# A ternary feed-forward kernel: low rank product in two bank pairs, copies and norms reordered, last rows by halves, masks of the second weight on GpSimd

## The reference

```python
def bitlinear(x, w):                       # per output row of w
    scale = clip(mean(abs(w), axis=1), 1e-5)
    tern = clip(round(w / scale), -1, 1)
    return x @ (tern * scale).T

def attn(x):       # 16 heads of 64, keys: 4 sinks and the last 512 tokens, causal against them
    w = softmax(where(cols <= rows + (t_ctx - t), q @ k.T / 8, -inf)); w = where(isnan(w), 0, w)
    return (w @ v) @ Wo

x = x + layernorm(attn(layernorm(x)))
h = bitlinear(layernorm(x), w_fc) + gate * (layernorm(x) @ v.T @ fast_b.T @ u.T)
x = x + layernorm(bitlinear(relu(h) ** 2, w_proj))
```

## Time and profile before

| | us |
|---|---|
| median of 3 runs | 1091.73 |
| lowest, highest | 1087.86, 1093.29 |
| the profiled execution | 1087.22 |
| its span, on the slowest of 8 cores | 1085.6 |
| spans of the other cores | 1078.3 to 1085.5 |

### The profile page before, as it was taken

How to read it: one execution, slowest core, us unless ns; L and a number is a source line. 1 busy time by engine, 2 the same in 40 slices (tenths; PEclk the granted TensorE clock), 3 DMA queues, 4 the chain that set the end, 5 groups by cost and what they waited for, 6 DMA issues and landing times.

```text
span 1085.6 us, 15004 instructions; the slowest of 8 cores (1078.3 to 1085.6 us)
## 1 busy us (share of the span) xinstructions
PE 1007.6 (93%) x4933; PEld 457.8 (42%) x4933; DVE 564.8 (52%) x817; ACT 362.4 (33%) x697; POOL 40.3 (4%) x97
## 2 busy tenths in 40 slices
PE   2789767999999899999999999999999989999997
PEld 1233233444444344544544444445444444444443
DVE  3877968744654553553445344633445354544333
ACT  4688787531002431134211341123310232014200
POOL 0101112000000000000000000000000000000000
PEclk9998889999999999999999999999999999999999
DMA  8799779841453314620445134522144301311021
GB/s 267 178 259 265 201 200 217 188 105 59 142 158 93 99 48 107 162 51 7 74 111 125 46 45 79 154 59 65 46 110 136 78 21 30 114 51 40 1 72 45
DMA packets 106223, 116.93 MB, mean 108 GB/s; under 512 B 82317, under 2 KB 82573, under 8 KB 106148
## 3 DMA queue, kind: packets, MB, share of 16 engines
q1 hardware_dynamic: 102180, 103.64, 36.9%
q0 software_dynamic: 3728, 12.25, 5.9%
q10 hardware_dynamic: 240, 0.07, 0.0%
HBM read 87.79 MB, written 17.31 MB: 97 GB/s over the span
## 4 chain that ended last, share of the span: by engine, by line
PE 81%; DVE 5%; DMA 5%; issue 4%; ACT 3%; SPq 1%; POOL 0%; ACTq 0%; DVEq 0%; POOLq 0%
PE pjp L635 37%; PE fcb L618 30%; PE pjp L618 3%; DVE below L1393 1%; PE xp L781 1%; PE xp L635 1%; PE xp L744 1%; PE pt L618 1%; PE fcb L635 1%; ACT rpp L1012 1%; PE xp L681 1%; DMA lrow<-ctx 1%; ACT absd L1052 1%; DMA stg<-wfc 1%; DMA r<-v 1%
## 5 line engine op out<-in xcount | busy, mean ns | idle before, releaser
L618 PE MATMUL fcb<-xnT,Sfc 128*128 128x512 bf16 x1792 | 408.0, 385 | 9.9 <-DVE r L1369 9.4
L635 PE MATMUL pjp<-Spj,r 128*128 128x512 fp8e4 x1664 | 366.8, 380 | 1.7 <-DVE r2b L1369 1.7
L618 PEld LDWEIGHTS fcb<-xnT,Sfc 128*128 128x128 bf16 x1792 | 172.2, 99 | 226.0 <-issue 34.4
L1369 DVE TENSOR_TENSOR r<-fcb,rpp 128x512 bf16<-128x512 f32 x192 | 131.3, 690 | 217.9 <-ACT rpp L1012 217.7
L635 PEld LDWEIGHTS pjp<-Spj,r 128*128 128x128 bf16 x1664 | 160.8, 98 | 195.9 <-issue 7.3
L1012 ACT ACTIVATE rpp<-fcb,hsc 128x512 f32<-128x512 f32 x192 | 130.4, 686 | 210.1 <-PE fcb L618 201.1
L975 ACT ACTIVATE lv<-mv,cvecs 128x1 f32<-128x1 f32 x64 | 18.8, 293 | 286.2 <-DVE mv L1342 206.5
L1332 DVE TENSOR_TENSOR xy<-pjp,oscb 128x512 f32<-128x512 f32 x60 | 41.3, 689 | 132.4 <-PE pjp L635 132.4
L635 PE MATMUL pjp<-Spj,r2b 128*128 128x512 fp8e4 x256 | 55.4, 379 | 0.0
L1337 DVE BATCH_NORM_STATS2 s<-xy 128x6 f32<-128x512 f32 x64 | 44.4, 694 | 9.4 <-DVE xy L1332 6.1
L618 PE MATMUL pjp<-xnT,Sfc 128*128 128x512 bf16 x176 | 41.9, 388 | 7.0 <-ACT xnT L992 3.7
(11 more groups left out here) (166 smaller groups left out, 681.5 us busy)
## 6 DMA issues: line engine op xcount, KB each, us to landing
out<-xy SPq DMA_DIRECT2D x32, 512.0 KB, 2.9
xy<-x SPq DMA_DIRECT2D x31, 512.0 KB, 4.5
xs<-x SPq DMA_DIRECT2D x25, 512.0 KB, 4.6
xy<-wfc SPq DMA_DIRECT2D x16, 512.0 KB, 5.8
xy<-wpj SPq DMA_DIRECT2D x15, 512.0 KB, 5.3
stg<-wfc SPq DMA_DIRECT2D x10, 512.0 KB, 6.4
stg<-wpj SPq DMA_DIRECT2D x9, 512.0 KB, 5.4
xs<-wpj SPq DMA_DIRECT2D x8, 512.0 KB, 5.0
```

Of the source, the lines that this page charges most:

```text
L618: mm = te.matmul(bank, s_fc[:, dci * HF + hc * 128:dci * HF + hc * 128 + 128], xnT[:, dci * TT:(dci + 1) * TT], start=(dci == 0), stop=(dc ...
L635: mm = te.matmul(dst, squares(j)[:, hc * TT + s * 128: hc * TT + s * 128 + 128], spj_even[:, hc // 2, hc % 2, half * 512:half * 512 + 512] ...
L1369: ve.tensor_tensor(squares(j)[:, hc * TT:(hc + 1) * TT], bank, rpp[n % 2][:], ALU.mult).then_inc(v_r2, 1)
```

## The change

- The low rank product alternates between `xp` and `pjp` by unit, so that it waits for the mask two units back and not for the last one. `low_rank(1)` moves ahead of `turn(3)`; TensorE's wait for all masks moves from row block 7 to 4, whose transposes use `pjp`.
- Tile 0: ScalarE takes `rstd1(3)` ahead of `turned(2)`, VectorE `cut(0)` between the statistics and the apply step of block 3.
- Tile 1: `turned(4)` to `turned(7)` move to the head of n = 33.
- Second weight: GpSimd's `under(n)` makes the mask of units 32 to 63, between its `group` calls, with a wait for the ternary step of unit n-2; VectorE waits for it.
- Ring: units from 49 on use slots 5 to 8 and 0 to 3, sums run 7 units ahead from 49 and 6 from 57; tile 1's chunks: 16 between n = 37 and 47, then 49, 51, 53, 55, and 56 to 59 as before.
- `stats` loses its wait; the apply steps `ln_end` and `residual_end` run from `attend_end`.
- Last block: VectorE normalises columns 0 to 511, ScalarE 512 to 1023, VectorE adds x by halves, SyncE stores by halves.

```diff
@@ -38,10 +38,9 @@
 NUNIT = NFU + NPU
 GRP = 4
 NSLOT = 9
-NRING9 = 58
-
-SLOT = [n % NSLOT if n < NRING9 else (6, 7, 8, 0, 1, 2)[n - NRING9]
-        for n in range(NUNIT)]
+
+SLOT = [n % NSLOT for n in range(49)] + [5, 6, 7, 8, 0, 1, 2, 3,
+                                         6, 7, 8, 0, 1, 2, 3]
 TURN_OF = [SLOT[:n].count(SLOT[n]) for n in range(NUNIT)]
 USERS = [[n for n in range(NUNIT) if SLOT[n] == k] for k in range(NSLOT)]
 AFTER = {n: m for u in USERS for n, m in zip(u, u[1:])}
@@ -53,14 +52,14 @@
 TURN_AT = [16 * len([m for m in range(n % 3, n + 1, 3) if m not in BY_PE])
            for n in range(NUNIT)]
 SUMS = [[u for u in range(8, NUNIT)
-         if u - (8 if u < NRING9 else 6) == n] for n in range(NUNIT)]
+         if u - (8 if u < 49 else 7 if u < 57 else 6) == n] for n in range(NUNIT)]
 CHUNKS = [[] for n in range(NUNIT)]
 for c in range(24):
-    CHUNKS[36 + 11 * c // 12 if c < 12 else 35 + c if c < 20 else 36 + c
+    CHUNKS[37 + 11 * c // 16 if c < 16 else 17 + 2 * c if c < 20 else 36 + c
            ].append(c)
 LATE = range(24, HCN)
 
-PLACE = {12: 49, 16: 50, 20: 58, 24: 63}
+PLACE = {12: 40, 16: 49, 20: 57, 24: 63}
 
 STATS = {25: 4, 26: 5, 27: 6, 28: 7}
 
@@ -133,6 +132,8 @@
         lv2 = sbuf("lv2", [128, NI], F32)
         rs1 = sbuf("rs1", [128, NI], F32)
         rs2 = sbuf("rs2", [128, NI], F32)
+
+        nmean = sbuf("nmean", [128, 2], F32)
         wsum = sbuf("wsum", [128, NUNIT], F32)
         thr = sbuf("thr", [128, NFU + OCN], F32)
         nthr = sbuf("nthr", [128, NFU + OCN], F32)
@@ -276,6 +277,7 @@
         g_us = sem("g_us")
         v_rt = sem("v_rt")
         g_own = sem("g_own")
+        g_be = sem("g_be")
         p_ut = sem("p_ut")
         a_ut = sem("a_ut")
         v_ab = sem("v_ab")
@@ -328,6 +330,8 @@
         v_y2 = sem("v_y2")
         a_y2 = sem("a_y2")
         v_out = sem("v_out")
+        v_nm = sem("v_nm")
+        a_half = sem("a_half")
         v_own = sem("v_own")
         a_own = sem("a_own")
 
@@ -468,9 +472,13 @@
                         attend(proj_step(j, s, 1))
                     if s < 3:
                         after_norm2(i + s)
-            after_norm2(NI - 1)
+            for half in range(2):
+                cols = slice(512 * half, 512 * half + 512)
+                sync.wait_ge(v_out, NI + half)
+                sync.dma_start(t_out[TOK - 128:TOK, cols], yy[1][:, cols]
+                               ).then_inc(d_out[1], 16)
             sync.wait_ge(d_out[0], 16 * (NI // 2))
-            sync.wait_ge(d_out[1], 16 * (NI // 2))
+            sync.wait_ge(d_out[1], 16 * (NI // 2) + 16)
 
 
         @block.gpsimd
@@ -532,10 +540,25 @@
                     gp.tensor_scalar(nthr[:, q:q + 1], thr[:, q:q + 1], -1.0,
                                      None, ALU.mult).then_inc(g_thr, 1)
 
+            def under(n):
+
+                c = NFU + (n - NFU) // GRP
+                gp.wait_ge(v_ab, n - 1)
+                gp.tensor_scalar(below[n % 2][:], stg[SLOT[n]][:],
+                                 nthr[:, c:c + 1], None, ALU.is_lt
+                                 ).then_inc(g_be, 1)
+
             gp.dma_start(identb[:], t_id[:, :]).then_inc(d_cst, 16)
             gp.wait_ge(d_us, 16)
-            for g in range((NFU + NPU) // GRP):
+            for g in range(NFU // GRP):
                 group(g)
+            group(NFU // GRP)
+            for n in range(NFU, NUNIT):
+                if n % GRP == 0:
+                    gp.wait_ge(g_thr, n // GRP + 1)
+                under(n)
+                if n % GRP == 2 and n + GRP < NUNIT:
+                    group(n // GRP + 1)
             gp.wait_ge(p_pj, 4 * NSUB)
             rows(0)
             gp.dma_start(mask[:], t_mw[:, :]).then_inc(d_msk, 16)
@@ -574,7 +597,7 @@
                 te.wait_ge(v_xn, i + 1)
                 if 0 < i < NSUB:
                     te.wait_ge(a_xt, i)
-                if i == NSUB + 3:
+                if i == NSUB:
                     te.wait_ge(v_lr, NFU)
                 if i == 2:
                     te.wait_ge(a_ut, 1)
@@ -675,10 +698,10 @@
                 g, k = divmod(n, GRP)
                 c = ((g % 2) * GRP + k) * 128
                 te.wait_ge(a_ut, g + 1)
+                if n > 1:
+                    te.wait_ge(v_lr, n - 1)
                 for half in range(2):
-                    if n > 0:
-                        te.wait_ge(v_lr, n)
-                    te.matmul(xh[half], uTs[0:16, c:c + 128],
+                    te.matmul((xh, pjb)[n % 2][half], uTs[0:16, c:c + 128],
                               gfold[0:16, half * 512:half * 512 + 512],
                               start=True, stop=True).then_inc(p_lr, 1)
 
@@ -907,8 +930,8 @@
             te.wait_ge(a_g, 1)
             low_rank(0)
             turn(2)
+            low_rank(1)
             turn(3)
-            low_rank(1)
             te.wait_ge(a_xt, NSUB)
             for n in range(NUNIT):
                 if n in BY_PE:
@@ -1212,14 +1235,17 @@
             sc.activation(gfold[:], pjp[0:16, :], AF.Copy,
                           scale=0.5).then_inc(a_g, 1)
             ut_copy(0)
+            rstd1(3)
             turned(2)
-            rstd1(3)
             abssum(4)
             turned(3)
             abssum(5)
             abssum(6)
             abssum(7)
             for n in range(NUNIT):
+                if n == HCN + 1:
+                    for i in range(NSUB, 2 * NSUB):
+                        turned(i)
                 for hc in CHUNKS[n - 1] if n > 0 else ():
                     second(hc)
                 if n in BY_PE:
@@ -1235,9 +1261,6 @@
                 if 3 <= n < HCN + 3:
                     relu(0, n - 3)
                     square(0, n - 3)
-                if n == HCN + 2:
-                    for i in range(NSUB, 2 * NSUB):
-                        turned(i)
                 if n > 1 and n % GRP == 0 and n + 4 < NFU:
                     ut_copy(n // GRP + 1)
             out_scale(1)
@@ -1267,6 +1290,13 @@
                     if j > 1:
                         attend(proj_step(j, s, 1))
             rstd2(NI - 1)
+            sc.wait_ge(a_y2, NI)
+            sc.wait_ge(v_nm, 1)
+            settled(sc.activation(nmean[:, 1:2], nmean[:, 0:1], AF.Copy,
+                                  scale=rs2[:, NI - 1:NI]))
+            sc.activation(yy[1][:, 512:1024], yy[1][:, 512:1024], AF.Identity,
+                          scale=rs2[:, NI - 1:NI],
+                          bias=nmean[:, 1:2]).then_inc(a_half, 1)
 
 
         @block.vector
@@ -1354,6 +1384,25 @@
                 ve.tensor_tensor(yy[i % 2][:], yy[i % 2][:], xr[i % 2][:],
                                  ALU.add).then_inc(v_out, 1)
 
+            def last_rows(i):
+
+                ve.wait_ge(v_y2, i + 1)
+                ve.tensor_scalar(nmean[:, 0:1], mv2[:, 2 * i:2 * i + 1], -1.0,
+                                 None, ALU.mult).then_inc(v_nm, 1)
+                ve.wait_ge(d_xr[1], 16 * (i // 2 + 1))
+                ve.wait_ge(a_y2, i + 1)
+                settled(ve.tensor_scalar(yy[1][:, 0:512], yy[1][:, 0:512],
+                                         mv2[:, 2 * i:2 * i + 1],
+                                         rs2[:, i:i + 1],
+                                         ALU.subtract, ALU.mult))
+                for half in range(2):
+                    cols = slice(512 * half, 512 * half + 512)
+                    if half == 1:
+                        ve.wait_ge(a_half, 1)
+                    ve.tensor_tensor(yy[1][:, cols], yy[1][:, cols],
+                                     xr[1][:, cols], ALU.add
+                                     ).then_inc(v_out, 1)
+
             def square(j, hc):
                 n = HCN * j + hc
                 ve.wait_ge(a_rl, n + 1)
@@ -1386,19 +1435,17 @@
                     ve.wait_ge(p_un, n // 4 + (n % 4 > 2))
                 elif n > 2:
                     ve.wait_ge(d_tr[n % 3], TURN_AT[n - 3])
-                if n > 1:
+                if 1 < n < NFU:
                     ve.wait_ge(v_ab, n - 1)
                 if n < NFU:
                     ve.wait_ge(p_lr, 2 * n + 2)
                     ve.scalar_tensor_tensor(
                         below[n % 2][:], stg[SLOT[n]][:], nthr[:, c:c + 1],
-                        xp[:], ALU.is_lt, ALU.subtract).then_inc(v_lr, 1)
+                        (xp, pjp)[n % 2][:], ALU.is_lt,
+                        ALU.subtract).then_inc(v_lr, 1)
                     ve.wait_ge(v_lr, n + 1)
                 else:
-                    settled(ve.tensor_scalar(below[n % 2][:],
-                                             stg[SLOT[n]][:],
-                                             nthr[:, c:c + 1], None,
-                                             ALU.is_lt))
+                    ve.wait_ge(g_be, n - NFU + 1)
                 dst, sat = ((tern[n % 3][:], None) if n < NFU else
                             (tern8[n % 3][:], False))
                 ve.scalar_tensor_tensor(dst, stg[SLOT[n]][:],
```

(30 more changed lines are left out.)

## The result

The changed kernel took **1103.36 us** in the median against 1091.73: ratio **1.0127** (95% interval 1.0102 to 1.0151), slower by 1.3% (the quotient of the two medians is 1.011). Medians are of all executions, ratios and intervals of those in which no die was slowed, so where versions are close the ratios decide. The forecast was 1094.1 with a range of 1085 to 1103 and half of the chance on no change. The direction was given 0.33, and the time lies just outside the range.

The account below looks back on a forecast made before the run. TensorE was taken to bound the kernel (93% busy) after a weight stage with other limits. From 1087.22 us, -3.6 (weight stage) +7.5 -1.0 -0.5 = +2.4 gave 1089.6, or 1094.1 on the median's scale; range 1085 to 1103.

Parts of the forecast that it names:

- The mask on GpSimd: Second weight's masks, units 32 to 63: 1.3 us each on GpSimd taken, bounds 0.75 and 1.7 us.
- Rival B: Second weight: GpSimd's mask is the new bound, 1.7 us each, T48 6.3 us later, total +8.8, 1100.5 us; chance 0.22.
- T48: The moment unit 48 starts the first products with the second weight, 188.55 us; a later one is lost one for one.
- Mask and ternary step one after the other: Second weight's units: GpSimd's mask cannot run beside VectorE's ternary step, so a unit costs 3.1 us.
- T48 stays: Weight stage: 16 units at 3.1 us from 134.3 end at 183.9, against 184.05 before, so T48 does not move.
- Cover of 15 us behind T48: Late second-weight units: last mask at 229, last weights wanted at 250.02, so about 15 us cover the ring's other shifts.
- Chunks and ring: Tile 1's products: 16 instead of 14 before T48, filling TensorE's holes; gain 2 x 1.73 = 3.5 us.
- Pairs: Low rank product in two bank pairs: 1.5 us gained, about 0.2 us for each of seven groups of four units.
- Copies first: Tile 1's row copies ahead of abssum(41): gain 0.4 us at most, 0 taken.
- Context norms: Apply behind the next square lengthens the loop through single buffer lrow to 10.4 us periods: loss 7.5 us, bounds 6 and 9.
- Rival D: Context norms lose nothing, as rows land early or the apply finds a hole: -5.1 us, 1086.6; chance 0.12.
- Residual and last rows: Attention residual norms in two parts gain 1.0 us; last rows by halves gain 0.5, ends -0.5 and 1.3.

Follow-up runs that it names:

- e1: The changed kernel with the masks of units 32 to 63 made by VectorE again: 1084.03 us, ratio 0.9931.
- e13: The kernel before with only the change's ring, places of the sums and chunk order: 1084.91 us, ratio 0.9949.
- e5: The kernel before with only the low rank product in two bank pairs and tile 0's reordering: 1090.57 us, ratio 0.9996.
- e4: The changed kernel with masks back on VectorE and context norms whole again, residual still split: 1076.72 us, ratio 0.9861.
- e6: e4 with the ring, sums and chunk list of the kernel before: 1087.51 us, ratio 0.9952.
- e9: The changed kernel, GpSimd's masks kept, with ring, sums and chunk order as before the change: 1099.72 us, ratio 1.0081.
- after: The kernel with the whole change, as against the kernel before: 1103.36 us, ratio 1.0127.
- e7: e4 with the four copies of tile 1's rows back behind relu(31): 1079.70 us, ratio 0.9893.
- e11: e1 (context norms in two parts) with two buffers for the context's rows: 1077.47 us, ratio 0.9881.
- e12: The changed kernel with VectorE making all masks and GpSimd doing three unread 320-column compares per mask place: 1134.55 us, ratio 1.0407.

## Why the prediction was wrong, by its own steps

**The mask on GpSimd: the step that failed.** It was sized from products of 4 and 64 columns, which gave 1.5 ns a column and 1.7 us as "upper bound"; measured, 2.84 us. Between 512 and 1024 columns the slope is 2.4 ns. At 4 and 64 columns most of the time is not the columns', so their difference of 0.09 us said little of it, and a bound taken from it was none. Rival B had the right cause, the mask as the new bound, with a price from the same rows (6.3 us, all of it ahead of T48); measured, T48 moved by 2 us and most of the rest came behind it, and the weight stage was 11.8 us worse than forecast. By the Trainium skill (GPSIMD Engine Reference, 4.1 Engine selection), one-input work is roughly at line rate there; the measured 2.84 us against VectorE's 0.75 says otherwise here. The prediction's 1.1 us is itself more than that rule gives: with the 1.2 GHz of the same page of the Trainium skill (1. Specifications) and one column a cycle, 1024 columns are 0.85 us, an estimate too.

**Mask and ternary step one after the other: wrong, and it hid the real limit.** The forecast summed 1.28 + 1.3 + 0.5 to a pace of 3.1 us a unit. With 2.84 that sum would be 4.6 us, but four units took 13.5 us, 3.4 each: the step runs inside the mask and loses 0.78 us. The small operations of the earlier trace rows do wait (1.14 us at 166.97 again), but a mask that has begun does not keep a whole ternary step out. The Trainium skill (SBUF — State Buffer, SBUF: two separate sides) states an exclusive lock for the whole instruction; the overlap from 158.30 to 160.37 disagrees for this pair. The right sum for that stretch was one of GpSimd's queue alone: 4 x 2.84 + 2.1 = 13.5 against 12.8 before.

**T48 stays: nearly, and by luck.** It moved by 2.0 us on the cores shown and by 1.9 in the median of eight (187.4 to 189.3). Without the masks it came at 183.3 (e1), so the rest of the change had given 4 us there, where the forecast saw 1.5, and the masks took 6. Which part gave them isn't settled: alone, ring and chunks moved T48 by 3.0 us (e13) and the pairs by 1.7 (e5), but ring and chunks taken out of e4 only by 0.8 (e6).

**Cover of 15 us behind T48: wrong.** The cover was read off the kernel before, where the last mask was made at 229 and the weights wanted at 250. It was taken for slack of a stage that would keep its pace. But the late chunks' squares stand on VectorE behind ternary steps that wait for masks, so a late mask stops TensorE long before the last weight is wanted: 8.5 us at 227.44, and 3.1 us of slow clock behind it, a term that the sum did not have. The prediction named the price of lost cover and not who is queued behind the waiting instruction. It also put the shorter ring at nothing; with GpSimd's masks it cost 4.5 us (e9 beside after).

**Chunks and ring: right.** 3.5 us forecast; 3.5 measured between T48 and the projection (58.0 against 61.5 us), and 4.6 by e6, 6.8 by e13 in the start of the projection (each to some 2.5 us). **Pairs:** 1.5 forecast, 1.6 in the profile of e5 and nothing in its time; not told from zero. That the waits for masks are not what bounds that stage was right. **Copies first:** 0 forecast, 1.2 by e7, not told from zero.

**Context norms: right in mechanism, near in size.** +7.5 forecast (6 to 9), +6.0 in the table and +7.2 core by core; the loop through the single buffer is shown by e11. The periods of the full row blocks were 9.3 to 10.4 us on the core shown, not 10.4 throughout, and the loads landed in 4.2 us, not 4.4. One sign failed: TensorE's waits were to be about 13 us and were 8.9, because part of the loss took the form of slow clock. Rival D fell with it.

**Residual and last rows: right.** The residual's waits went from 3.6 to 2.1 us (-1.5, forecast -1.0); last product to end from 7.8 to 7.1 us (-0.7, forecast -0.5).

**Range.** It ended at 1103.0 because B was priced at 1.7 us a mask. With 2.84 in the same reasoning it would have reached well beyond. Unlike the sum, it had no need of a good estimate of the mask, only of a bound that was one.

## What to carry to other kernels

Work moved to an idle engine is to be weighed against the pace of its queue, not against the engine's share of the span: here 12% busy in the mean was 95% in the stretch, with the next group's thresholds behind the masks in the same queue. Where no row shows an operation at its size on the new engine, a slope between two tiny ones bounds nothing; take a wide range, or ask at which price the plan turns over (here 12.8 us for four masks and a threshold chain, 2.7 us a mask) and whether you know that it lies below. And splitting a step pays only where nobody waits for its second half: behind a single load buffer somebody did.

## What the hardware showed that was not expected

A compare of 128x1024 float32 to bfloat16 with a column of thresholds took 2.84 us on GpSimd and 0.75 on VectorE; 512 columns took 1.62 on GpSimd, and 320 columns 1.08 when VectorE stood still. A ternary step of VectorE that began just behind such a compare took 2.06 instead of 1.28 us, and the compare kept its 2.84, but for one of 32. TensorE's granted clock fell to 0.5 for 3.4 us behind waits of 2.66 and 2.60 us at 370 and 391 us, and not behind those of 1.26 and 0.92 in the same stretch, nor behind the 3.00 us ahead of T48. Beside VectorE's masks and ternary steps in a row both paid, GpSimd more: the 320 columns took up to 2.3 us in e12, VectorE's masks 0.95 and its ternary steps 1.30:

```profile
154.36 2.04 POOL L549 TENSOR_SCALAR shd<-identf,nthr 128x320 bf16<-128x320 f32 x1 [0.29 <-POOL shd L549]
...
161.15 1.08 POOL L549 TENSOR_SCALAR shd<-identf,nthr 128x320 bf16<-128x320 f32 x1 [0.17 <-POOL shd L549]
```

Why the late starter is delayed by only 0.78 us in one case and held until the step's end in the other stays open. The version without GpSimd's masks and with the context norms whole, 1076.72 us, is the fastest that was run, together with those that have two row buffers.
